# Split loads, per-batch quantized projections and bf16 sums in a four-layer Perceiver kernel

## What is computed

```python
# sublayer 1
scores = jnp.einsum('bsd,bmd->bsm', hidden_states, memory_tokens) * scale
scores = jnp.where(memory_mask[:, None, :], scores, neg_inf)
readout = jnp.einsum('bsm,bmd->bsd', softmax(scores), memory_tokens)
valid_b = jnp.any(memory_mask, axis=-1)          
# sublayer 6
xn = x / rms
w_ternary = clip(round(weight / (gamma + EPS)), -1, 1)     # gamma: mean |weight| of a row
x_q = clip(round(xn / (x_scale + EPS)), -127, 127)
out = einsum('bsk,nk->bsn', x_q, w_ternary) * gamma[:, 0] * x_scale + bias
# sublayer 7, around its attention
qx, sx = _dyn_quant(x); qw, sw = _quant_weight(w)
y = einsum('bnc,oc->bno', qx, qw) * (sx * sw[:, 0]) + b
# sublayer 12: operands rounded to float8_e4m3, results bf16
activations = gelu(x @ w_gating[0]) * (x @ w_gating[1]); out = activations @ w_linear
```

## Time and profile before

| | us |
|---|---|
| median of 3 runs | 1271.64 (1271.54 to 1272.27) |
| the profiled execution | 1273.29 |
| its span | 1271.1 |
| TensorE matmul busy | 1108.4 (87%) |
| TensorE weight load busy | 840.2 (66%) |
| VectorE busy | 675.0 (53%) |
| ScalarE busy | 524.7 (41%) |
| GpSimd busy | 204.3 (16%) |

### The profile page before, as it was taken

The page is one execution under the profiler, slowest core; times in us unless marked ns, Lnnn a source line. Parts: engine busy times, 40 slices in busy tenths (PEclk is TensorE's granted clock), DMA queues, the critical chain, the costliest instruction groups (busy, mean ns, idle before and its releaser), DMA issues.

```text
span 1271.1 us, 22592 instructions
## 1 busy us (share of the span) xinstructions
PE 1108.4 (87%) x9168; PEld 840.2 (66%) x9168; DVE 675.0 (53%) x1357; ACT 524.7 (41%) x947; POOL 204.3 (16%) x258
## 2 busy tenths in 40 slices
PE   2988889998999736999955889999999999999885
PEld 1565568874656514776644567778888888887763
DVE  5345242237888355888633536464445354555366
ACT  1122221114666404888713234444444344444264
POOL 0700148100020010000010121002001123322030
PEclk8998899998999857999967889999999999999997
DMA  9511146562553640000030111113111111200000
GB/s 396 214 54 60 61 159 216 174 190 87 163 159 101 213 147 2 2 2 2 2 133 1 34 53 32 34 34 116 35 34 51 51 51 51 75 18 9 1 1 9
DMA packets 35650, 102.44 MB, mean 81 GB/s; under 512 B 3808, under 2 KB 12256, under 8 KB 33248
## 3 DMA queue, kind: packets, MB, share of 16 engines
q1 hardware_dynamic: 31360, 88.91, 20.9%
q0 software_dynamic: 2752, 9.44, 2.3%
q10 hardware_dynamic: 1440, 2.70, 0.6%
HBM read 85.83 MB, written 15.20 MB: 79 GB/s over the span
## 4 chain that ended last, share of the span: by engine, by line
PE 80%; DVE 10%; ACT 3%; issue 3%; DMA 2%; POOL 1%; SPq 0%; POOLq 0%; DVEq 0%; ACTq 0%
PE ps L1967 10%; PE ps L1916 9%; PE ps L395 7%; PE ps L1554 5%; PE ps L1312 5%; PE ps L1950 5%; PE ps L1812 4%; PE ps L1821 4%; PE ps L388 4%; PE ps L449 3%; PE ps L1545 3%; PE ps L1394 3%; PE ps L1405 2%; DMA vv<-ctx_in 2%; PE ps L988 2%
## 5 line engine op out<-in xcount | busy, mean ns | idle before, releaser
L1967 PE MATMUL ps<-vv,probT 128*128 128x128 f32 x1024 | 135.3, 275 | 0.2 <-ACT probT L2032 0.2
L1967 PEld LDWEIGHTS ps<-vv,probT 128*128 128x128 f32 x1024 | 124.4, 192 | 0.5 <-ACT probT L2032 0.5
L2032 ACT COPY probT<-ps 128x512 f32<-128x512 f32 (+1 forms) x96 | 45.7, 478 | 122.2 <-PE ps L1950 118.6
L2066 ACT ACTIVATE prob<-ps,st,small 128x1024 f32<-128x1024 f32 x64 | 80.0, 1254 | 31.0 <-DVE st L2111 31.0
L1489 DVE TENSOR_REDUCE st<-ps 128x1 f32<-128x512 f32 x128 | 82.4, 685 | 19.3 <-PE ps L1394 13.0
L1950 PE MATMUL ps<-const,prob 128*128 128x128 f32 x544 | 85.6, 273 | 0.0
L1462 ACT ACTIVATE prob<-ps 128x1024 f32<-128x1024 f32 x64 | 65.5, 1025 | 47.8 <-PE ps L1407 29.2
L1854 DVE TENSOR_REDUCE small<-vv 128x4 f32<-128x512 f32 x32 | 21.9, 685 | 117.2 <-ACT vv L1837 117.2
L395 PE MATMUL ps<-xT,big 128*128 128x256 f32 x352 | 79.7, 380 | 1.6 <-ACT big L1004 0.7
L1950 PEld LDWEIGHTS ps<-const,prob 128*128 128x128 f32 x544 | 64.2, 141 | 16.7 <-issue 16.4
L395 PEld LDWEIGHTS ps<-xT,big 128*128 128x128 f32 x352 | 66.5, 190 | 11.9 <-ACT big L1004 1.1
(11 more groups left out here) (421 smaller groups left out, 2244.7 us busy)
## 6 DMA issues: line engine op xcount, KB each, us to landing
big<-blocks_in SPq DMA_DIRECT2D x22, 768.0 KB, 4.3
big<-ctxT_in SPq DMA_DIRECT2D x32, 512.0 KB, 4.1
key_parts<-w POOLq DMA_DIRECT2D x16, 384.0 KB, 4.1
kt<-key_parts SPq DMA_DIRECT2D x32, 192.0 KB, 3.2
vv<-ctx_in SPq DMA_DIRECT2D x2, 2176.0 KB, 21.4
vv<-early_values SPq DMA_DIRECT2D x4, 1088.0 KB, 12.5
kt<-ctxT_in SPq DMA_DIRECT2D x2, 2048.0 KB, 16.8
kt<-key_parts SPq DMA_DIRECT2D x32, 128.0 KB, 3.1
```

What stands on the lines that cost most here:

```text
L1967: last = pe.matmul(k.ps[:, 7, 0:P], k.probT[:, ch * P:ch * P + P], v, start=(ch == 0), stop=(ch == MC))
L2032: copy(k.probT[:, lo:hi], k.ps[:, 5 + t % 2, 0:hi - lo]).then_inc(s(copied), 1)
L2066: act.activation(self.prob(u)[:, lo:hi], k.bank(0, hi, 5)[:, lo:hi], ACT.Exp, bias=self.bias[:, i:i + 1], scale=self.scale[b][:, j:j + 1], ...
```

## The change

1. Loads: keys of batch 0, mask8, w2, keys of batch 1, values 0, quant, values 1, w0. Keys and values get a semaphore per batch; TensorE waits for keys before a batch's scores and for values before its products, GpSimd's split for the batch that it reads.
2. Whether any key is kept is counted by ScalarE (a copy of the mask with an accumulator) and tested on VectorE later. The weights of the projections are scaled on VectorE in seven parts between the `probT` copies; they are turned on TensorE between early pieces 1 and 2. Banks and buffers follow (`factors` in `k.big`).
3. `Norm`: `xn` is signalled per batch, and turned per batch. Statistics of a batch can be made right behind its residual.
4. `Quant`: activations, turns, casts, matmuls (banks 7 and 4, 6 and 5) and results go per batch; rounding's subtraction of MAGIC is in ScalarE's cast; two products are one op; for n=0 the root is folded into the scale. `bv` is added in each group of four heads in `n2` (64 columns), not behind it.
5. `Eight.hidden`: the sum is kept in bf16 (with a multiplier of 1.5 * 2^4 instead of 1.5 * 2^20).
6. Semaphores `e3_q`, `e3_lam_exp` and `e3_sb` are joined into one.

In the diff `keys(b)` and `values(b)` issue the loads of `ctxT[b]` and `ctx[b]`; `finish(b)` adds att to x and makes the statistics for n=0 and n=2, and adds `bq` for n=1.

```diff
 @block.sync
+            keys(0)
+            sp.dma_start(k.mask8[:, :], dram["mask8"]).then_inc(s("mask8_in"), 16)
+            sp.dma_start(k.w2.ap, dram["w2"]).then_inc(s("w12_in"), 16)
+            keys(1)
+            values(0)
             sp.dma_start(k.qz[:, 0:6 * D], dram["quant"]).then_inc(s("quant_in"), 16)
+            values(1)
             sp.dma_start(k.w0.ap, dram["w0"]).then_inc(s("w0_in"), 16)
 @block.tensor
             Norm.tensor(k, pe, 0)
-            Quant.weights_tensor(k, pe)
-            pe.wait_ge(s("quant_ready"), 1)
             pe.wait_ge(s("xT"), 1)
-            pe.wait_ge(s("context_in"), 64)
-            pe.wait_ge(s("bias_epsilon"), 1)
             c0.tensor(pe)
             early.tensor(pe, 1)
+            Quant.weights_tensor(k, pe)
             early.tensor(pe, 2)
+            pe.wait_ge(s("quant_ready"), 1)
 Cross.tensor
+                    pe.wait_ge(k.s(f"context_keys{j}"), 16)
...
+                    pe.wait_ge(k.s(f"context_values{j - 1}"), 16)
 Cross.scalar
+            act.wait_ge(k.s("mask8_in"), 16)
+            for b in range(B):
+                act.activation((self.prob(1), k.probT[:, 0:M])[b], k.mask8[:, b * M:(b + 1) * M], ACT.Copy,
+                               accum_out=k.st[:, 22 + b:23 + b]).then_inc(k.s("kept"), 1)
 Cross.vector
                         dve.tensor_copy(k.probT[:, lo:hi], k.ps[:, 5 + t % 2, 0:hi - lo]).then_inc(self.s("probT"), 1)
+                        Quant.weights_vector(k, dve, o, (j - 1) * self.turns + t)
 Norm.tensor
-        pe.wait_ge(k.s("norm_xn"), n + 1)
-        turn(k, pe, k.xn, 7).then_inc(k.s("norm_turned"), 1)
+        for b in range(B):
+            pe.wait_ge(k.s("norm_xn"), 2 * n + b + 1)
+            last = turn_batch(k, pe, k.xn, b, 7, b * D)
+        last.then_inc(k.s("norm_turned"), 1)
 Quant.weights_tensor
         pe.wait_ge(s("quant_w"), 1)
+        pe.wait_ge(s("early_copied"), 2)
...
+        pe.wait_ge(s("c_finished"), 2 + B)
+        pe.matmul(k.ps[:, 6, :], k.const("ones"), Quant.factors(k)[:, 0:512], start=True, stop=True)
 Quant.vector
+        o.step(dve.tensor_reduce(top, src, AX.X, ALU.max, apply_absolute_value=True))
+        if n == 0:
             dve.wait_ge(s("sum_roots"), 4)
-            o.step(dve.tensor_tensor(src, src, bc(k.st[:, 38:40], 2, D), ALU.mult))
+            rs = k.st[:, 38:40]
+            o.step(dve.scalar_tensor_tensor(sx, top, 1.0 / 127.0, rs, ALU.mult, ALU.mult))
             o.step(dve.tensor_scalar(div, sx, 1e-8, None, ALU.add))
+            o.step(dve.reciprocal(div, div))
+            o.step(dve.tensor_tensor(div, div, rs, ALU.mult))
         else:
+            o.step(dve.tensor_scalar(sx, top, 1.0 / 127.0, 1e-8, ALU.mult, ALU.max))
+            o.step(dve.reciprocal(div, sx))
-        o.step(dve.tensor_tensor(q, src, bc(div, 2, D), ALU.mult))
-        o.step(dve.tensor_scalar(q, q, MAGIC, -MAGIC, ALU.add, ALU.add))
-        dve.tensor_scalar(q, q, 127.0, -127.0, ALU.min, ALU.max).then_inc(s("quant_x"), 1)
+        for b in range(B):
+            o.step(dve.tensor_scalar(q[:, b], src[:, b], div[:, b:b + 1], 127.0, ALU.mult, ALU.min))
+            dve.tensor_scalar(q[:, b], q[:, b], -127.0, MAGIC, ALU.max, ALU.add).then_inc(s("quant_x"), 1)
+        if bias is not None:
+            o.step(dve.tensor_tensor(k.x, k.x, bc(bias, 1, B), ALU.add))
-        o.step(dve.tensor_tensor(q, y, bc(sx, 2, D), ALU.mult))
-        o.step(dve.tensor_tensor(q, q, bc(k.qwrow[:, n], 1, B), ALU.mult))
+        for b in range(B):
+            dve.wait_ge(s("quant_y"), 2 * n + b + 1)
+            o.step(dve.scalar_tensor_tensor(q[:, b], k.ps[:, Quant.MADE[b], 0:D], sx[:, b:b + 1], k.qwrow[:, n], ALU.mult, ALU.mult))
+            finish(b)
 Quant.scalar
-        act.wait_ge(k.s("quant_turned"), n + 1)
-        act.copy(flat(k.xq), k.bank(7)).then_inc(k.s("quant_xq"), 1)
+        for b in range(B):
+            act.wait_ge(k.s("quant_turned"), 2 * n + b + 1)
+            act.activation(k.xq[:, b].rearrange("p c t -> p (c t)"), k.ps[:, Quant.TURNED[b], 0:D], ACT.Copy, bias=-MAGIC
+                           ).then_inc(k.s("quant_xq"), 1)
 Keys.normalize
+        if self.layer:
+            o.step(last)
+            last = dve.tensor_tensor(out, out, k.w2("bv")[:, g % 4 * 64:g % 4 * 64 + 64], ALU.add)
 Split.gpsimd
-        pool.wait_ge(s("context_in"), 64)
         for n in range(first, last):
             i, b, c = self.BLOCKS[n]
+            pool.wait_ge(s(f"context_keys{b}"), 16)
 Eight
-        self.act = pieces(k.vv[:, 2048:4096])
+        self.sum16 = pieces(k.vv[:, 2048:3072].bitcast(BF16))
 Eight.hidden
-        o.step(self.multiple(dve, t))
+        o.step(dve.tensor_scalar(t, t, 2.0 ** -6, 1.5 * 2.0 ** 4, ALU.max, ALU.mult))
         o.step(dve.tensor_tensor(a, h, t, ALU.add))
```

More of the change, by code:

```diff
@@ L167, in vector, with stats, scaled @@
     @staticmethod
+    def stats(k, dve, o, b):
+        o.step(dve.bn_stats(k.st[:, 6 * b:6 * b + 6], k.x[:, b]))
+    @staticmethod
     def vector(k, dve, o, n):
+        for b in range(B):
+            Norm.stats(k, dve, o, b)
+        Norm.scaled(k, dve, o, n)
+    @staticmethod
+    def scaled(k, dve, o, n):
         st = k.st[:, 0:16]
-        for b in range(B):
-            o.step(dve.bn_stats(st[:, 6 * b:6 * b + 6], k.x[:, b]))
         mv = k.st[:, 16:20].rearrange("p (b s) -> p b s", b=B)
@@ L863, in weights_vector, with factors @@
     @staticmethod
-    def weights_vector(k, dve, o):
+    def factors(k):
+        return k.big[:, 10816:10816 + 6 * P]
+    @staticmethod
+    def weights_vector(k, dve, o, part):
         s = k.s
@@ L883, in weights_vector @@
-        dve.sem_inc(s("quant_w"), 1)
+        if part == 0:
+            dve.wait_ge(s("quant_in"), 16)
+            o.step(dve.tensor_reduce(sc[:, 0:2], raw[:, 0:2], AX.X, ALU.add, apply_absolute_value=True))
+        elif part == 1:
+            o.step(dve.tensor_reduce(sc[:, 2:6], raw[:, 2:6], AX.X, ALU.max, apply_absolute_value=True))
+        elif part == 2:
+            o.step(dve.tensor_scalar(sc[:, 0:2], sc[:, 0:2], 1.0 / D, None, ALU.mult))
+            o.step(dve.tensor_scalar(sc[:, 2:6], sc[:, 2:6], 1.0 / 127.0, 1e-8, ALU.mult, ALU.max))
+            o.step(dve.tensor_scalar(div[:, 0:2], sc[:, 0:2], 1e-8, None, ALU.add))
+            o.step(dve.tensor_copy(div[:, 2:6], sc[:, 2:6]))
+        elif part == 3:
+            dg = Quant.factors(k).rearrange("p (w n) -> p w n", w=6)
+            o.step(dve.tensor_tensor(dg, bc(k.const("ident"), 1, 6), bc(sc, 2, P), ALU.mult))
+            o.step(dve.reciprocal(div, div))
+        elif part == 4:
+            o.step(dve.tensor_tensor(raw, raw, bc(div, 2, D), ALU.mult))
+        elif part == 5:
+            o.step(dve.tensor_scalar(raw, raw, MAGIC, -MAGIC, ALU.add, ALU.add))
+        elif part == 6:
+            o.step(dve.tensor_scalar(raw[:, 0:2], raw[:, 0:2], 1.0, -1.0, ALU.min, ALU.max))
+            o.step(dve.tensor_scalar(raw[:, 2:6], raw[:, 2:6], 127.0, -127.0, ALU.min, ALU.max))
+            dve.sem_inc(s("quant_w"), 1)
@@ L901, in weights_scalar, with vector @@
         act.wait_ge(s("quant_t"), 1)
-        act.copy(flat(k.qw), k.bank(1, 1536, 3))
-        act.copy(flat(k.qwrow), k.bank(4, 768, 2)).then_inc(s("quant_ready"), 1)
+        act.copy(flat(k.qw), k.bank(3, 1536, 3))
+        act.copy(flat(k.qwrow), k.bank(6, 768, 2)).then_inc(s("quant_ready"), 1)
+    TURNED, MADE = (7, 4), (6, 5)
     @staticmethod
-    def vector(k, dve, o, n, src):
+    def vector(k, dve, o, n, src, bias, finish):
         s = k.s
-        sx, div = k.small[:, 336:338], k.small[:, 338:340]
+        top, sx, div = k.small[:, 324:326], k.small[:, 336:338], k.small[:, 338:340]
         q = k.att
@@ L912, in vector @@
             for b in range(B):
-                o.step(dve.tensor_tensor_reduce(out=q[:, b], in0=src[:, b], in1=src[:, b], scale=1.0, scalar=0.0,
-                                                op0=ALU.mult, op1=ALU.add, accum_out=k.st[:, 36 + b:37 + b]))
+                last = dve.tensor_tensor_reduce(out=q[:, b], in0=src[:, b], in1=src[:, b], scale=1.0, scalar=0.0,
+                                                op0=ALU.mult, op1=ALU.add, accum_out=k.st[:, 36 + b:37 + b])
+            o.step(last)
@@ L935, in gpsimd, with add, finish @@
+    @staticmethod
+    def add(k, dve, o):
+        def finish(b):
+            o.step(dve.tensor_tensor(k.x[:, b], k.x[:, b], k.att[:, b], ALU.add))
+            Norm.stats(k, dve, o, b)
+        return finish
     @staticmethod
@@ L2538, in _ @@
             Norm.scalar(k, act, 0)
-            Quant.weights_scalar(k, act)
             c0.scalar(act)
@@ L2542, in _ @@
             early.scalar(act, 1)
+            Quant.weights_scalar(k, act)
             early.scalar(act, 2)
@@ L2639, in _ @@
             Norm.vector(k, dve, o, 5)
-            dve.wait_ge(s("norm_xn"), 6)
-            Quant.vector(k, dve, o, 0, k.xn)
-            o.step(dve.tensor_tensor(k.x, k.x, bc(k.w1("bias"), 1, B), ALU.add))
```

(17 more changed lines are left out.)

103 lines of the change are left out of this document (42 added, 61 removed).

## The result

| | before | changed |
|---|---|---|
| median, us (4 runs each) | 1271.95 (1271.54 to 1273.77) | 1244.13 (1241.47 to 1245.86) |
| profiled execution | 1273.29 | 1243.74 |
| its span | 1271.1 | 1241.8 |
| granted TensorE clock | 0.935 | 0.946 |
| TensorE matmul busy | 1108.4 | 1104.5 |

What follows compares the result with a forecast made beforehand. TensorE held 80% of the chain that ended last, so time was to leave mainly where it waits. Start 14.3, projections 10.0, norms 2.0 and tail 2.0 sum to 28.3 us; 1271.64 less that gives 1243.3, range 1237 to 1250.

Steps and rivals of the forecast that it cites:

- Start: Program start: scores start 18.4 us earlier, less 3.1 for weights' turns and 1.0 for VectorE-GpSimd contention, saving 14.3.
- A part of up to 1.5 is free: VectorE's weight scaling between probT copies: a part of up to 1.5 us fits in TensorE's round at no cost.
- all later stages hang on this one by semaphores and move along: After the start: every later stage keeps its length, so the start's 14.3 us gain carries through.
- Quantized projections: Three quantized passes with batches overlapped and operations merged: 4.1, 2.35 and 3.5 us saved, together 10.0.
- Rival (b): Quantized projections: handing over by halves costs as much as by wholes; they give 5, total 1248.3; chance 0.11.
- Norms: Turn of batch 0 starts 0.33 us earlier at norms 2, 4, 7, 8, 9 and 10, saving 2.0.
- Tail: Last layer's hidden pieces: two 512-wide ops each become all-bf16, 0.42 instead of 0.69 us, saving 2.0.
- (a): Program start: second keys or weights parts come later than forecast; the start gives 9, total 1248.6; chance 0.15.
- (c): MoE stage: TensorE's 5.09 us block wait may go, total 1238.2, or double, total 1248.4; chance 0.12.
- (d): Program start: some semaphore still waits for the last values; scores start 23.0 us later, total 1266.3; chance 0.03.
- (e): TensorE, started early with gaps for loads, stays at 1.2 GHz instead of 2.4; up to 1279.3; chance 0.02.
- three things named as signs of an error: Wrong if first scores start after 14 us, batch 0 probT copies over 3 apart, or a quantized pass over 9.

Runs made afterwards that it cites:

- after_again: The changed kernel run once more, unedited; measured 1243.81 us.
- split_four_early: The changed kernel with four of GpSimd's 16 split steps ahead of the mLSTM block instead of six; measured 1245.12 us.
- old_load_order: The changed kernel with its waits on parts, but the loads in the order of the kernel before; measured 1259.23 us, ratio 0.9882 against the kernel before.
- wait_for_all: The changed kernel, but TensorE waits for all four context loads before the first scores; measured 1267.48 us, ratio 0.9969 against the kernel before.

## Why the prediction held

The time was 1244.13 against 1243.3, for the reasons given in four of its parts, and by luck in the way the rest cancelled.

**Start, 14.3 forecast, 16.6 and 17.6 measured at norm 2 in the two executions.** The order and the waits do what was said. At the mLSTM block's first turn the gain was 12.9 and 14.4. Four terms differ. (1) Keys 0 landed at 10.8, not 11.8, and the first scores started at 10.95, not 12.1: 19.6 instead of 18.4. In the other executions with the new order of loads they started between 10.0 and 11.8, so about 1 us of this is scatter. The second keys, put at 22.4 to 24.2, were there by 21.5. (2) The weights on TensorE: 2.6 for 3.1. (3) VectorE's parts and the lock: 2.0 in the profiled execution (1.0 at the sum of x and att, 1.0 between the copies of batch 1) and 1.8 in the next, for 1.0, inside the ends of 0 and 3. "A part of up to 1.5 is free" was right (L911 with 1.19 held nothing up), but "under that but for one product" was not with the lock: L911 reached 1.88, and L913 and L914, one part, took 2.0 together, 1.1 without it. L909 takes 1.75 unlocked, which the round as good as covers. (4) The clock: in the profiled execution TensorE's products of batch 0 took 9.7 at a granted clock of 0.82, where the next had 8.1 at 1.00; from the mLSTM block's turn to norm 2 the two took 3.7 and 3.2 less than the kernel before, with 0.97 and 0.93 granted in its longest part, where the kernel before had 0.88. Neither was in any term: the step that failed is "all later stages hang on this one by semaphores and move along". They move along, but not at the same speed.

**Quantized projections, 10.0 forecast, 10.2 measured**: 4.20 for 4.1, 2.41 for 2.35, 3.58 for 3.5. Costing each operation by its nearest row worked to 0.1 per pass. Operations from SBUF to SBUF with a scalar from a tile came at 0.35 instead of 0.41, from PSUM at 0.48 instead of 0.54; the two-way overlap was 1.7 for 1.75. Rival (b) is excluded: handing over by halves costs TensorE 0.16 and 0.10 more per pass (1.12 and 1.01, now 1.28 and 1.11).

**Norms, 2.0 forecast, 1.7 measured**: 0.32 at four of them, 0.22 and 0.23 at norms 10 and 2.

**Tail, 2.0 forecast, 2.4 measured.** I had let ScalarE's deliveries hold the last pieces back; one held the third by under 0.2, the fourth was held by none.

**The rest.** The causal attention lost 3.5 in this execution, which after_again did not. Norm 7 to 8 won 2.0 beyond its norm, with a granted clock of 0.88 against 0.80; split_four_early and old_load_order, which have the same code there, took 37.98 and 37.97 at 0.80, as good as the 38.35 of the kernel before. So neither is a term of the change that holds in every execution. Terms against measurement: start +2.3, causal attention -3.5, norms 7 to 8 +2.0, tail +0.4, projections +0.2, norms -0.3: 28.3 + 1.1 = 29.4, by the landmarks 29.3. Between these two executions, then, the forecast was 1 us short; it could as well have been off by 3 with the same reasoning.

**Rivals.** (a) Late starts: the second keys came in time and VectorE's parts and the lock cost 2 in all, not 5. (c) The MoE stage kept its length (row norm 3 of the table by stage), block waits of 5 us included. (d) is the experiment wait_for_all, at 1267.5 where I had put 1266.3. (e) As put, it is wrong: from the second scores to the mLSTM block the granted clock was 1.00 but for the products of batch 0 (0.82). But the mechanism is real elsewhere: behind the norms and the quantized passes TensorE runs at 1.2 GHz in both kernels (0.50 from 446.0 to 463.4 in the changed one, 0.50 from 459.4 to 474.1 before), and filling the waits gave each some 20 us. The prediction read the half clock off single durations and kept those durations; it did not ask what filling the waits would give.

Of the three things named as signs of an error one came about: probT copies of batch 0 at 35 and 38 were 3.4 apart in the profiled execution (34.50 and 37.88). It was the clock, granted at 0.70 and 0.50 between them, and not the parts: in the next execution, with the same parts, they are 2.0 apart. The other landmarks stand at 23.99 (25.2), 45.97 and 43.75 (44 to 45) and 67.30 and 65.84 (65 to 66).

## What to carry to other kernels

Order loads by the first instruction that reads them, in every engine's program: what cost most under the old order was a weight load that nobody was thinking of. Measure a small edit at its own stage, between two landmarks, and not by the total, when the total of one kernel scatters by more than the edit is worth. And look at the granted clock behind TensorE's waits: work that fills the wait can be worth more than shortening it, as here 20 us against 10 for three rewritten projections.
